# Self-attention of a decoder layer: other slots for the next rows' and residuals' loads, and for ScalarE's copies of the lent rows

## What is computed

```python
Wdkv = x @ latent_w + latent_b                                   # 72 latent columns, keys and values at once
q = jnp.einsum('btc,hcl->bhtl', x, Wd_w) + Wd_b[None, :, None, :]  # 16 heads
scores = jnp.einsum('bhtl,bsl->bhts', q, Wdkv) / jnp.asarray(np.sqrt(d_head), dtype=x.dtype)
scores = jnp.where(causal[None, None, :, :], scores, -jnp.inf)
attn = jax.nn.softmax(scores, axis=-1)
y = jnp.einsum('bhts,bsl->bhtl', attn, Wdkv)
z = jnp.transpose(y, (0, 2, 1, 3)).reshape(b, t, h * Wdkv.shape[-1])
return z @ out_w + out_b
```

## Time and profile before

| | |
|---|---|
| median of 3 runs | 3077.07 us (3076.62 to 3077.79) |
| the profiled execution | 3077.02 us, span of its trace 3075.3 us |
| self-attention in the trace | 0 to some 1149 us |
| PE busy over the span | 3045.8 us, 99% |
| granted TensorE clock | 0.999 |

### The profile page before, as it was taken

How to read it: one execution, slowest core, us unless ns; L and a number is a source line. 1 busy time by engine, 2 the same in 40 slices (tenths; PEclk the granted TensorE clock), 3 DMA queues, 4 the chain that set the end, 5 groups by cost and what they waited for, 6 DMA issues and landing times. The chain is left out here.

```text
span 3075.3 us, 72559 instructions
## 1 busy us (share of the span) xinstructions
PE 3045.8 (99%) x22401; PEld 2859.5 (93%) x22401; DVE 2252.8 (73%) x6595; ACT 2163.8 (70%) x6949; POOL 1554.1 (51%) x2854
## 2 busy tenths in 40 slices
PE   9999999999999999999999999999999999999998
PEld 7999999999999989999999999999988888889998
DVE  7888888888888877787888778888765554454665
ACT  8888888888888878888888888888744444442222
POOL 5677666666666664333333333333556666652000
PEclk9999999999999999999999999999999999999999
DMA  5556555555455561111112111111354454534333
GB/s 172 147 157 170 164 164 164 155 136 136 128 141 134 132 201 46 46 56 56 46 50 65 46 49 63 46 47 55 111 137 102 99 118 104 113 51 97 123 123 103
DMA packets 206753, 326.82 MB, mean 106 GB/s; under 512 B 36417, under 2 KB 137409, under 8 KB 205409
## 3 DMA queue, kind: packets, MB, share of 16 engines
q1 hardware_dynamic: 177376, 277.82, 30.0%
q0 software_dynamic: 24576, 33.57, 6.5%
q10 hardware_dynamic: 4480, 11.54, 2.0%
HBM read 125.20 MB, written 75.50 MB: 65 GB/s over the span
## 5 line engine op out<-in xcount | busy, mean ns | idle before, releaser
L1229 POOL TENSOR_SCALAR ca_prob<-ca_prob,ca_inverse 128x120 f32<-128x120 f32 x1024 | 355.1, 366 | 623.3 <-DVE ca_inverse L1554 621.3
L888 ACT ACTIVATE sa_prob<-sa_prob,sa_shift 128x128 f32<-128x128 f32 (+1 forms) x1024 | 453.7, 461 | 0.0
L1495 ACT ACTIVATE ca_prob<-bank,ca_shift 128x120 f32<-128x120 f32 x1024 | 353.2, 364 | 1.7 <-DVE ca_shift L1548 0.4
L601 POOL TENSOR_SCALAR sa_prob<-sa_prob,sa_inverse 128x128 f32<-128x128 f32 x512 | 198.3, 387 | 228.2 <-DVE sa_inverse L961 215.6
L949 DVE CUSTOM_DVE_ANT_0 sa_prob<-bank,sa_mask 128x128 f32<-128x128 f32 (+1 forms) x1024 | 303.8, 351 | 1.7 <-issue 0.7
L139 PE MATMUL bank<-sa_kvT_b,sa_q 112*128 112x128 f32 (+1 forms) x1024 | 260.7, 280 | 0.0
L996 DVE TENSOR_TENSOR sa_pT_lo<-bank,sa_pT_hi 128x384 fp32r<-128x384 f32 x512 | 258.2, 544 | 0.2 <-ACT sa_pT_hi L877 0.2
L137 PE MATMUL bank<-sa_kvT_a,sa_q 128*128 128x128 f32 (+1 forms) x1024 | 250.3, 280 | 4.1 <-DMA sa_q<-sa_q_tile 2.8
L603 POOL TENSOR_SCALAR sa_prob<-sa_prob,sa_inverse 128x256 f32<-128x256 f32 x512 | 248.6, 486 | 0.0
L1988 POOL DMA_INDIRECT mid_acc<-ex_out,ex_to_tokens x112 | 192.5, 1719 | 98.7 <-DVE ex_out L2300 66.6
L989 DVE TENSOR_TENSOR sa_y_lo<-bank,sa_y_hi 72x512 fp32r<-72x512 f32 x256 | 174.6, 682 | 76.7 <-ACT sa_y_hi L869 73.8
(11 more groups left out here) (274 smaller groups left out, 11698.9 us busy)
## 6 DMA issues: line engine op xcount, KB each, us to landing
sa_q<-sa_q_tile SPq DMA_DIRECT2D x125, 288.0 KB
sa_q<-sa_q_tile SPq DMA_DIRECT2D x157, 112.0 KB
mid_x2T<-ca_x2T SPq DMA_DIRECT2D x32, 512.0 KB, 3.0
ex_sx<-mid_x2T SPq DMA_DIRECT2D x32, 512.0 KB
sa_q<-sa_q_tile SPq DMA_DIRECT2D x297, 32.0 KB
sa_y_lo<-sa_y_lo ACTq DMA_DIRECT2D x96, 96.0 KB
sa_xT_raw<-in_xT SPq DMA_DIRECT2D x32, 256.0 KB, 3.9
sa_q<-sa_q_tile SPq DMA_DIRECT2D x32, 256.0 KB
```

The costliest lines, as they stand in the source:

```text
L601: pool.tensor_scalar(prob[:, r, hh, 0:P], prob[:, r, hh, 0:P], inverse[:, r, 2 * hh:2 * hh + 1], 1.0, ALU.mult, ALU.mult)
L888: act.activation(prob[:, r, hh, cols], prob[:, r, hh, cols], ACT.Exp, bias=shift[:, r, n:n + 1], scale=-1.0, accum_out=total[:, r, n:n + 1 ...
L1229: ins = pool.tensor_scalar(prob[:, r, t, hh], prob[:, r, t, hh], inverse[:, r, n:n + 1], 1.0, ALU.mult, ALU.mult)
L1495: act.activation(prob[:, r, t, hh], SC[g % 2][:, n * S:n * S + S], ACT.Exp, bias=shift[:, r, n:n + 1], accum_out=total[:, r, n:n + 1]).the ...
```

## The change

Three numbers in the tables move, and one special case goes:

- `xT_raw` of the next group is loaded in u = 3 instead of u = 1 (it was u = 3 already for the very first load). In u = 3 it stands behind tile 1's pieces.
- `x_res` is loaded in u = 4 and 5 of the following group (as it was already in the first one) instead of u = 0 and 1.
- `LEND`: n = 1, 2 of the first lenders go out in u = 12 instead of 13, n = 3 in u = 13 instead of 15; of the second lenders n = 1, 2 stay in u = 4, n = 3 goes out in u = 5 instead of 7.

```diff
-    X_NEXT, X_FIRST, X_SPLIT = 1, 3, (8, 11)
+    X_NEXT, X_SPLIT = 3, (8, 11)
...
-    RES_FIRST, RES_IN, RES = (GROUP + 4, GROUP + 5), (GROUP, GROUP + 1), (GROUP + 6, GROUP + 9)
-    LEND = {13: (2, (1, 2)), 15: (4, (3,)), 4: (1, (1, 2)), 7: (4, (3,))}
+    RES_IN, RES = (GROUP + 4, GROUP + 5), (GROUP + 6, GROUP + 9)
+    LEND = {12: (1, (1, 2)), 13: (2, (3,)), 4: (1, (1, 2)), 5: (2, (3,))}
...
-            if u == (X_FIRST if first_body(J) and c == 0 else X_NEXT) and group_exists(J, c + 1):
+            if u == X_NEXT and group_exists(J, c + 1):
...
-            for c, i in due(J, m, RES_FIRST if first_body(J) and m < 2 * GROUP else RES_IN):
+            for c, i in due(J, m, RES_IN):
```

## The result

The changed kernel takes 3097.34 us (median of 6 runs, 3092.74 to 3100.29) against 3077.43 us before (6 runs beside it): a ratio of 1.0059, 95% interval 1.0048 to 1.0070. It is slower by 15 to 22 us, and the forecast of 3079.4 us was wrong in size: 3097.34 lies 10 us above the upper end of its range. The profiled execution of after took 3100.29 us, with a span of 3098.5 us, the longest of the six; its span is 23.2 us longer than that of before (3075.3).

A forecast was written before the change was run, and what follows sets the result against it. The PE was taken as the bound (99% busy), stalling mainly in slot 6 for q tile 1. Part 2's +3.5 us and the last body's -1.1 gave +2.4 on 3077.02: 3079.4 us, range 3074.5 to 3087.5.

The forecast's parts named there:

- What bounds the kernel: PE 99% busy; slot 6 waits for q tile 1, 4.8 us in total; about 7 us at most to win.
- Part 2, the transfer: n = 3 copy beside tile 1's last pieces, slot 5: 0.2 us a group, bounds 0 and 0.48.
- The upper case of the transfer: Each packet of the n = 3 copy goes in front of tile 1's last ones: 15 x 0.48 = +7.2 us.
- Part 2, the issue: SP's issue of tile 1 beside ACT's n = 3 copy in slot 5: 0.1 us a group, bound +0.56.
- Part 1, the loads: xT_raw and x_res loads moved behind tile 1, slots 3 to 5: 0, up to +0.2 us a group.
- in time by 0.4 us: Tile 2, queued behind the moved loads, still reaches the PE for slot 8 with 0.4 us of room.
- Part 3, the first lenders: Copies moved to slots 12 and 13: q tile 0 to 0.2 us late, covered by 0.54 us; sum 0.
- Part 4, the last body: Last lent copy lands earlier, so y_lo of slot 8 starts earlier: 1.07 us of the PE's 1.81 won.
- Tile 1 is delayed by more than half a microsecond: Rival, slot 6: lent copy's packets go in front; at 0.7 us a group +8.4 us, 3085.5 us; 15%.
- ACT late in slot 12: Rival: copies wait for slot 11's exponentials, 0.73 us x 15 = 11 us, 3088 to 3090 us; 8%.
- tile 1 not delayed: Rival, slot 6: the copy fits into DMA gaps, only -1.1 us is left, 3076.0 us; 22%.
- the loads as the trouble of slot 6: Rival: without loads at the group's start all slot 6 stalls go, -4.8 - 1.1, 3071 us; 5%.

The follow-up runs named there:

- e4: The kernel before with only n = 3 of the second lenders moved from slot 7 to slot 5: 3088.14 us, ratio 1.0034 to before.
- e1: The kernel before with only the xT_raw and x_res loads moved, LEND as before: 3083.91 us, ratio 1.0016 to before.
- e5: The kernel before with a semaphore of its own for the two pieces of tile 1 that slot 6 reads: 3070.86 us, ratio 0.9979.
- e10: The kernel before with only the first lenders' copies moved, to slots 12 and 13: 3078.33 us, ratio 1.0006 to before.
- e2: The kernel before with the whole of LEND changed and the loads left in slots 0 and 1: 3092.53 us, ratio 1.0045 to before.

## Why the prediction was wrong, point by point

The step that failed is part 2's transfer. The prediction took 0.2 us a group for it, 0.3 with the issue and +3.5 us in all; the copy alone cost 0.69 us a group on the way to the PE, 0.79 us of stall, and 10.5 us of time (e4). Two terms that it put at nothing come on top: the loads, 2 to 8 us (e1), and the clock, 4.2 us in the profile of after.

- **What bounds the kernel.** Right in place, and all hung on it: slot 6 waits for tile 1, every group stood on the edge, and e5 won what I had put at most for it (4.8 us) and a little more: the "clean" groups hid 0.13 us each, and in the last body the PE's stall of 1.81 us is 1.13 in e5. The 0.2 us to spare that I gave the five groups without a stall was not there: in e4 they stall for 0.90 to 1.24 us.
- **Part 2, the transfer, was mis-sized.** I bounded it by 0 and 0.48 us and took 0.2, because the engines were only 0.57 busy there. Measured: 0.69 us more from the last issue to the PE, 0.79 us of stall a group (e4). Both the value and the bound failed. The bound took the mean of all copies, spread over 16 engines; for this one, on 12, the same working gives 0.70. And a share of 0.57 told nothing of gaps on the engines and at the moment that mattered. The upper case of the transfer, each packet in front (+7.2 us), was nearer than the sum, and still too low; e4 agrees with the rule beside it, that of the Trainium skill ("DMA: Bandwidth & Descriptors", section "Issuing engines are not separate DMA queues"), that DMAs started by SP and by ACT interleave on the same 16 engines. Part 2's bound with the issue, 1.04 us a group and +15.6 us, did hold e4's 0.79. The range did not keep it: its upper end, 3087.5, is 10.4 us above before, and so below part 2's own bound.
- **Part 2, the issue.** I took 0.1 us; the mean end of SP's issue moved by 0.07 us in e4, within what chance does. Right, but its bound of 0.56 rested on a wrong contrast: the copies of 0.74 us were not "alone", SP was issuing beside them too (at 1001.26 beside the copy of 1001.22). The copy came 0.45 us behind the start of the `y_hi` of slot 4 in group 14 of after (1013.72 to 1014.17) and 0.77 behind it in group 10 of e4 (719.28 to 720.05), where I had written 0.78: in any case among tile 1's last pieces.
- **Part 1, the loads.** I took 0 with 0.2 us a group as the bound. In slot 6 they cost 0.15 us a group (e1). The step that failed here is tile 2: "in time by 0.4 us" used the way of 2.9 us from a group without staged weights, and "the 768 KB pass in about 3 us" left out that in the early groups 768 KB of weights stand with them. There tile 2 is issued 0.74 us later and takes 6.2 us to the PE (e1, group 5). By time e1 costs 0.06 to 0.25%, 2 to 8 us.
- **Part 3, the first lenders.** The cover of 0.54 us held: no wait in slot 13, and e10 costs 0.06% (-0.04 to 0.15%).
- **Part 4, the last body.** -1.07 us forecast, 1.81 to 0.73 measured, -1.08.
- **The clock was not priced.** A stall was taken to cost its own length. With those of groups 7 and 13 of after, 2.99 and 1.73 us, the clock fell and cost 2.8 and 1.5 us more. It may be part of the spread of after's runs as well: spans of 3091.0 and 3091.1 us at a mean clock of 0.999 and 0.998, 3097.7 and 3098.5 us at 0.997.
- **The rivals.** "Tile 1 is delayed by more than half a microsecond" was the right one, at 15% and 0.7 us a group, which would have given 3085.5 us. (By its own sum it decides from 0.55 us a group on, not from 0.52.) With 0.79 us in all 15 groups (11.9), the loads (4.9 by e1's ratio) and -1.1 it is 3092.7, the lowest of after's runs; the clock brings up to 4.2 more. The other rivals fell: ACT late in slot 12 (e10), tile 1 not delayed (e4), and the loads as the trouble of slot 6 (e1, where taking them away from slots 0 and 1 gained nothing).

**Left open.** In the profiles of e2 and e10, the two kernels that move the first lenders' copies without the loads, group 15 has a stall of 2.82 and 1.52 us in slot 6 against 0.30 before, with some of SP's pieces issued far slower there: the first of tile 1 in 1.52 and 1.37 us (0.54 before), the fifth in 1.76 and 1.15 (0.69 before). These are rows of e10 (timeline of SP and PEld):

```profile
1058.84 1.37 SPq L536 DMA_DIRECT2D sa_q<-sa_q_tile  x1
...
1062.58 1.15 SPq L543 DMA_DIRECT2D sa_q<-sa_q_tile  x1
...
1068.68 0.19 PEld L137 LDWEIGHTS bank<-sa_kvT_a,sa_q 128*128 128x128 f32 x1 [1.52 <-issue]
```

The late end of SP's issue, by 1.76 and 0.97 us against before, makes the greater part of the longer stalls. Such slow issues are not peculiar to these kernels: between 60 and 1120 us the trace of before has 36 single issues of SP of 1.2 us or more, e2 24 and e10 30. What makes an issue slow is not shown, nor whether it is chance that they fall there; after itself has 1.40 us in that group. Nor is it shown why group 7's stall in after (2.99 us) is about twice the others': SP ends tile 1 there 21.64 us after the start of the group, earlier than in the mean (22.07), and the way to the PE is 5.37 us.

## What to carry to other kernels

Before moving a transfer, ask which semaphore is the tight one and what it counts: here the PE waited for eight pieces and read two, and a semaphore of its own for the two made some 17 us of the change's cost vanish and gave 0.21% on the kernel before. Where a chain ends on the edge of a wait, price a small copy put beside its last transfers at its full length on the engines that it uses, once a group: here it cost 0.69 us, and the working done afterwards gives 0.70, although the DMA engines had been at 0.57 there. And look at all the tiles that are queued behind a moved issue, in the groups in which other work stands there too.

## What the runs showed of the hardware

- A copy of 24 partitions and 96 KB, 0.52 us of all 16 DMA engines by the queue's total, delayed what waited for other DMAs in flight by 0.69 us behind their last issue; half of it by 0.25 us.
- Of ACT's copies that are issued while SP issues too, a lone one takes 0.77 us, and the third of three in a row 1.30; in the mean of 15 groups before that third one takes 1.27 us in slot 4. In slots 13 and 14, where SP issues little beside the first two, the third takes 0.75. Why is not shown.
- With waits of the PE the granted clock fell to the 1.2 GHz level (0.50) in some groups and not in others. In after it did with a wait of 2.99 us (0.50 from 515 to 521) and one of 1.73 (0.50 from 949 to 951, 1.00 from 952 on), and did not with three of 1.85 to 2.06 us. In e2 and e4 the windows of ten microseconds that hold the ends of waits of 1.94, 2.82 and 1.95 us have 0.83; before has 1.00 in its window of group 1. The length of the wait alone does not tell. The rows are of after (group 13) and of e4 (group 1):

```profile
949.00:950.00 1.00, 1.00 (x3) 0.79 (x3) 0.00 (x0) 0.00 (x0) 0.81 (x3) 0.50 0.82 186
```

```profile
80.00:90.00 10.00, 8.22 (x40) 6.99 (x39) 7.07 (x27) 7.01 (x23) 5.32 (x13) 0.83 0.69 203
```
